# Two of a pixel's 36 deformable samples made on TensorE instead of one, their per-token rows spread over the partitions by transposes instead of by a trip through DRAM

## The reference, cut to what matters

```python
def bilinear_sample(img, iy, ix, H, W):
    x0, y0 = jnp.floor(ix), jnp.floor(iy)
    wx1, wy1 = ix - x0, iy - y0
    ...
    return corner(y0, x0, (1 - wy1) * (1 - wx1)) + corner(y0, x0 + 1, (1 - wy1) * wx1) \
         + corner(y0 + 1, x0, wy1 * (1 - wx1)) + corner(y0 + 1, x0 + 1, wy1 * wx1)
...
samp = bilinear_sample(img, iy, ix, Hin, Win).reshape(N, GROUP, H, W, P, Cg)
y = jnp.einsum('nghwpc,nhwgp->nhwgc', samp, mask_sm)      # P = 9 samples, masks by softmax
```

## Time and profile before

| | us |
|---|---|
| median of three runs | 8871.78 |
| the profiled execution | 8856.78 |
| its span in the profile | 8855.0 |
| TensorE matmul busy | 5535.4 |
| VectorE busy | 5200.9 |
| ScalarE busy | 2368.2 |
| GpSimd busy | 6546.0 |

### The profile page before, as it was taken

One profiled execution on the slowest core, in us unless ns is written; L12 is line 12 of the kernel. 1 busy time (PEld: TensorE's weight loads), 2 busy tenths in 40 slices (PEclk: granted clock), 3 DMA queues, 4 the chain that ended last, 5 costly groups with the idle time before them and its releaser, 6 DMA issues.

```text
span 8855.0 us, 69949 instructions
## 1 busy us (share of the span) xinstructions
PE 5535.4 (63%) x19826; PEld 3066.5 (35%) x19826; DVE 5200.9 (59%) x10762; ACT 2368.2 (27%) x5042; POOL 6546.0 (74%) x6899
## 2 busy tenths in 40 slices
PE   4547575656765577566675567664767566664567
PEld 2224343333432334333333334332433333332334
DVE  4655656556565655666475656655656655655553
ACT  2223222222332233222222222222323222222222
POOL 6777777777777777777777777777777777777771
PEclk7768787777877788777887778876878777776778
DMA  7323333233333323333233323333233323222220
GB/s 104 77 70 70 73 70 78 66 75 70 70 77 69 76 66 73 76 73 71 68 75 72 74 68 72 74 75 69 67 78 71 76 66 65 73 65 65 62 64 15
DMA packets 851804, 624.52 MB, mean 71 GB/s; under 512 B 551035, under 2 KB 734563, under 8 KB 851473
## 3 DMA queue, kind: packets, MB, share of 16 engines
q0 software_dynamic: 221200, 452.53, 21.1%
q1 hardware_dynamic: 629600, 167.72, 11.4%
q10 hardware_dynamic: 672, 0.24, 0.0%
HBM read 549.38 MB, written 70.57 MB: 70 GB/s over the span
## 4 chain that ended last, share of the span: by engine, by line
POOL 57%; issue 21%; PE 12%; DVE 6%; DMA 3%; SPq 1%; ACT 1%; POOLq 0%; DVEq 0%; another core or an unknown queue 0%; ACTq 0%
POOL ring L715 57%; PE bank L1466 2%; PE bank L1500 2%; PE bank L1488 2%; DMA ring<-column_table,idx_r 2%; DVE y L1042 2%; PE bank L1394 1%; PE bank L1651 1%; PE bank L1628 1%; DVE ring L1032 1%; PE bank L1563 1%; SPq L530 1%; DMA tokens<-z 0%; SPq L500 0%; DMA tin<-tokens 0%
## 5 line engine op out<-in xcount | busy, mean ns | idle before, releaser
L715 POOL DMA_INDIRECT ring<-column_table,idx_r x6860 | 6521.9, 951 | 2129.6 <-issue 2069.1
L1032 DVE TENSOR_TENSOR ring<-ring,bank 128x4608 f32<-128x4608 f32 x196 | 970.3, 4950 | 1189.4 <-POOLq L726 1188.2
L1042 DVE TENSOR_REDUCE y<-ring 128x128 f32<-128x4608 f32 x196 | 1572.9, 8025 | 24.3 <-remote 22.3
L1455 PE MATMUL bank<-ident,xh 112*128 112x112 f32 x224 | 56.4, 407 | 1317.0 <-DVE xh L962 1317.0
L1466 PE MATMUL bank<-kT,qT 128*112 128x448 f32 (+3 forms) x1792 | 812.8, 601 | 98.4 <-DVE cmax L1141 62.9
L1152 DVE RECIPROCAL rinv<-bank 112x2 f32<-112x2 f32 x112 | 18.5, 165 | 1307.0 <-PE bank L1513 1307.0
L1500 PE MATMUL bank<-pT,xh 112*128 112x448 f32 (+3 forms) x1792 | 774.2, 514 | 17.6 <-ACT pT L836 15.8
L1488 PE MATMUL bank<-qT,kT 128*112 128x448 f32 (+3 forms) x1792 | 750.4, 504 | 1.2 <-ACT qT L830 1.2
L836 ACT ACTIVATE pT<-bank 112x448 f32<-112x448 f32 (+3 forms) x896 | 451.7, 506 | 820.6 <-PE bank L1488 642.3
L1563 PE MATMUL bank<-xpad,diag 128*128 128x448 f32 x1008 | 492.0, 652 | 235.2 <-ACT xflat L853 184.1
L1141 DVE TENSOR_REDUCE cmax<-bank 112x1 f32<-112x448 f32 (+3 forms) x896 | 506.1, 579 | 187.3 <-PE bank L1466 94.3
(11 more groups left out here) (187 smaller groups left out, 7061.6 us busy)
## 6 DMA issues: line engine op xcount, KB each, us to landing
ring<-column_table,idx_r POOLq DMA_INDIRECT x6860
xflat<-dense_rows SPq DMA_DIRECT2D x56, 406.0 KB
column_table<-proj SPq DMA_DIRECT2D x196, 112.0 KB
corner_weight<-wts_s SPq DMA_DIRECT2D x56, 252.0 KB, 4.5
wts_r<-corner_weight SPq DMA_DIRECT2D x196, 72.0 KB
hT<-dense_rows SPq DMA_DIRECT2D x224, 56.0 KB
tin<-tokens SPq DMA_DIRECT2D x56, 224.0 KB, 3.1
out<-xn SPq DMA_DIRECT2D x56, 224.0 KB
```

What stands on the lines that cost most here:

```text
L715: pool.indirect_dma_start(ring[:, r, e * CORNERS:(e + 1) * CORNERS, :].rearrange("p s c -> p (s c)"), None, source, bass.IndirectOffsetOnA ...
L1032: dve.tensor_tensor(corners, corners, wts_p.unsqueeze(2).broadcast_to([128, GP * CORNERS, CG]), ALU.mult)\
L1042: dve.tensor_reduce(y[:, k % BLK % 2].rearrange("p (g c) -> p g c", g=G), ring[:, bass.ds(t % RING, 1)].rearrange("p o (g e) c -> p (o g) ...
```

## The change

FETCHED goes from 35 to 34 and DENSE = 2 samples of a pixel are made from image rows on TensorE, both of group 3. Ring buffers shrink to 136 corners. The multiply covers 128 x 4352 elements, and the sum is split in two instructions, groups 0 to 2 and group 3 with its 7 gathered samples. The trip through DRAM is gone (`store_rows`, `load_rows` and their semaphores): `drow` becomes a ring of LEAD = 8 chunks, `spread_rows` makes 16 transposes of single columns read with stride zero over 116 columns, and `widen_weights` (ScalarE) with `spread_weights` (TensorE, 4 transposes a sample) and `keep_weights_spread` (ScalarE) put the row weights on 128 partitions in `part`. There are now 10 items of two hats and two matmuls instead of 5. `keep_part` moves from `experts_front` to the end of `attention`.

```diff
-FETCHED = GP - 1
+DENSE = 2
+FETCHED = GP - DENSE
+STAGES = NB // 2
+ITEMS = DENSE * STAGES
 def hats_ahead(j):
-    return min(NB // 2 - 1, 2 + j)
+    return max(STAGES, ITEMS + 1 - blocks(j))
 # SyncE
-    load_rows(i, j, gd, fronts)          # in mlp
-    store_rows(i, j)                     # in front
 # ScalarE
+def widen_weights(gd, d):
+    act.wait_ge(d_placed, FIRST + gd + 1)
+    act.activation(t1[:, :, :].rearrange("p t (r c) -> p t r c", r=DY),
+                   drow[:, gd % LEAD, d, :, 2:].unsqueeze(3).broadcast_to([TT, NT, DY, CG]), ACT.Copy)
+def keep_weights_spread(p, f, d):
+    ...
+    act.activation(part[:, f % 2, d], bank[WEIGHT_BANK][:, 0:CH], ACT.Copy).then_inc(d_weights_kept, 1)
+    if d + 1 < DENSE:
+        widen_weights(gd, d + 1)
 # ScalarE, attention
-    for stage in range(ahead):
-        hats(gd, stage)
+    widen_weights(gd, 0)
+    for item in range(ahead):
+        hats(gd, item)
 ...
+    if now and b < DENSE:
+        keep_weights_spread(*now, b)
-    if now and 1 <= b <= NB // 2 - ahead:
+    if now and 1 <= b <= ITEMS - ahead:
         hats(gd, ahead + b - 1)
 # VectorE
+    for d in range(DENSE):
+        step.did(dve.tensor_scalar(place[d], bank[PLACE_BANKS[d][0]][0:2 * PAD, 0:CH], ...))
+    for d in range(DENSE):
+        step.wait()
+        ins = dve.scalar_tensor_tensor(place[d], place[d], -1.0, bank[PLACE_BANKS[d][1]][0:2 * PAD, 0:CH], ...)
-    if now: keep_part(*now)              # experts_front, behind the layer norm
+    if now: keep_part(*now)              # attention, ahead of the reads of o_projected; now two multiplies
 # TensorE
+def spread_rows(gd):
+    for d in range(DENSE):
+        for r in range(2):
+            for t in range(NT):
+                ins = pe.transpose(bank[PLACE_BANKS[d][r]][0:2 * PAD, t * TT:(t + 1) * TT],
+                                   rows[:, d, t, r:r + 1].broadcast_to([TT, 2 * PAD]), ident[0:TT, 0:TT])
+def spread_weights(gd, d):
+    for t in range(NT):
+        ins = pe.transpose(bank[WEIGHT_BANK][:, t * TT:(t + 1) * TT], t1[:, t, :], ident[0:TT, 0:TT])
 # TensorE, attention
     banks_left(fronts, s * 2 + h, g)
+    spread_rows(gd)
 ...
+    pe.wait_ge(d_placed, FIRST + gd + 1) # ahead of the scores
     for q in range(NT):
         ...                              # scores of q
-    sum_columns(di, gd, 0)
+        sum_columns(di, gd, q)
 ...                                      # row of maxima
-    for stage in range(1, ahead): sum_columns(di, gd, stage)
+    spread_weights(gd, 0)
+    for item in range(NT, ahead): sum_columns(di, gd, item)
 ...                                      # in the loop of turned scores, at block b
-        if now and 1 <= b < NB // 2 - ahead:
+        if now and 1 <= b <= ITEMS - ahead:
             sum_columns(di, gd, ahead + b - 1)
-    sum_columns(di, gd, NB // 2 - 1)     # behind the loop
+        if now and b + 1 < DENSE: spread_weights(gd, b + 1)
```

More of the change, by code:

```diff
@@ L154, in build @@
         stripes = sb("stripes", [2 * PAD, NB, DY * CG])
[L155 to L164, removed]
+        drow = sb("drow", [TT, LEAD, DENSE, NT, ROWS_KEPT])
+        dtmp = sb("dtmp", [TT, 4, DENSE, NT])
+        dint = sb("dint", [TT, DENSE, NT], I32)
+        part = sb("part", [128, 2, DENSE, CH])
+        wqT, wkT, wv_row = (part[:, 0, 0, k * C:(k + 1) * C] for k in range(3))
+        wqT_less, wkT_less = (part[:, 1, 0, k * C:(k + 1) * C] for k in range(2))
+        place = [hT[0:2 * PAD, d] for d in range(DENSE)]
+        ring = sb("ring", [128, RING, FETCHED * CORNERS, CG])
         x0 = ring[0:TT].rearrange("p r e c -> p (r e c)")[:, 0:NJ * NT * C]\
@@ L532, in load_stripes @@
                                      .rearrange("k x d -> x k d")).then_inc(d_stripes_in, 16)
[L534 to L543, removed]
-                sp.sem_inc(passed, 1)
-                sp.dma_start(xflat[0:2 * PAD].rearrange("p a n -> p (a n)"),
-                             row_d[gd, 0:2].rearrange("a n -> (a n)").partition_broadcast(2 * PAD)).then_inc(d_rows_in, 16)
-                for dy in range(DY):
-                    sp.dma_start(row_wts[dy * CG:(dy + 1) * CG], row_d[gd, 2 + dy].partition_broadcast(CG))\
-                        .then_inc(d_rows_in, 16)
             def dense(now):
-                load_rows(*dense_chunk(*now), (0, LEAD))
+                pass
             def first_image():
@@ L1148, in attention @@
                     sum_up(*second)
+                if now:
+                    keep_part(*now)
                 for a in range(2):
@@ L1398, in dense @@
                 i, _, gd = dense_chunk(*now)
-                for stage in range(NB // 2):
-                    sum_columns(i, gd, stage)
+                banks_left((0, LEAD), 0, 0)
+                spread_rows(gd)
+                for item in range(ITEMS):
+                    sum_columns(i, gd, item)
+                for d in range(DENSE):
+                    spread_weights(gd, d)
                 pe.wait_ge(d_kept, FIRST + gd + 1)
@@ L1479, in attention @@
                 if now:
-                    for stage in range(1, ahead):
-                        sum_columns(di, gd, stage)
+                    spread_weights(gd, 0)
+                    for item in range(NT, ahead):
+                        sum_columns(di, gd, item)
                 pe.wait_ge(row_kept, FIRST + g + 1)
```

163 lines of the change are left out of this document (97 added, 66 removed).

## The result

The changed kernel takes 8631.43 us, the median of 4 runs (8628.62 to 8636.41); the kernel before, beside it on the same chip, 8870.35 (8860.55 to 8876.0). The profiled execution took 8630.16 us, its span is 8628.4. All ratios here leave out two runs that lay far above the others of their kernel (12,087 us in experiment 4, 15,765 us in experiment 6).

The account below looks back on a forecast made before the run. The prediction took GpSimd's gathers, 188 tiles plus a tail, as the bound: 8855 - 235 + 22 + 1 = 8643 us for the span, -212; off the median, 8871.8 - 212 = 8660. Range 8640 to 8740.

Parts of the forecast that it names:

- 188 gathers at 1.25 us: GpSimd's stream: one gather fewer in each of the 188 tiles that count saves 235 us; by the reported span, 179.
- The tail, +22: From VectorE's last gather wait, tile 187, to the end: two dense chunks at +11.5 and +10.5 us; from +10 to +34.
- the places ahead of it: `set_places` on VectorE, ahead of the scores: reads PSUM, twice, 2.1 to 2.5 us instead of 1.1, so +1.4.
- The cover at tile 31: GpSimd's margin before tile 31: of 36 us, less some 3 for landing, 1 to 2 remain; waits +1 us in all.
- The copy's 4.2 us from the early `keep_part`: ScalarE's copy of the turned input, in fronts of 6 of 7 chunks, starts 4.2 us sooner without waiting for `keep_part`.
- VectorE's waits 330: VectorE's total wait for gathers over the kernel falls from 1188 us to some 330.
- What a tile costs beside its gathers (1.257 against 1.25 a gather) stays.: GpSimd's stream: the time per tile beyond its gathers' pitch was taken as unchanged.
- -10 us at an image's first chunk: SyncE's queue: without the removed loads, about 10 us (0 to 11) of VectorE's 13.26 us wait goes; the stripes stay.
- Taken off the median, 8871.8 - 212 = 8660.: Whole kernel: the -212 us change of the span was applied to the median, the profiled execution lying 15 us below it.
- a hidden tail: Rival: the first item falls into VectorE's lag at the scores' start; tail +5, no wait, 8643 us; chance 0.08.
- waits at tile 31: Rival: cover gone, waits of 6 to 26 us at tiles 31, 80, 129; 8680 to 8740 us; chance 0.27.
- The slow rival: ScalarE paces the loop and the engines behind the gathers become the bound: 25 us a chunk, 9067 us; chance 0.03.

Follow-up runs that it names:

- experiment 4: Changed kernel with one sample of a pixel from image rows and 35 gathered, by the new route: 8838.06 us, ratio 0.9972 to the kernel before.
- experiment 6: Twelve runs of variants of the changed kernel under conditions where every kernel took 13.9 to 14.6 ms; ratios to the kernel before from 0.9751 to 1.0245.
- Experiment 5: Changed kernel with 33 gathers a tile, sample 33 left out and its ring place zeroed once: 8447.92 us, ratio 0.9538 to the kernel before.
- experiment 3: Changed kernel with parts of the removed DRAM trip issued again, results unused: store alone 8678.82 us, ratio 0.9778; loads alone, from the input, 8650.65 us, ratio 0.9743.
- the whole trip: Changed kernel with the DRAM trip's store and loads issued again, result unused, and VectorE's wait for the store: 8691.35 us, ratio 0.9795 to the kernel before.

## Why the prediction was wrong, step by step

**Right.** *188 gathers at 1.25 us.* The spacing is 1.249 in the traces of before and after, and -234.8 us stands in the difference. The span (0.95 us) would have given 179; the gathers' start-to-start spacing is what counts.

*The tail, +22.* It is +22.5, and the tail of the kernel before, profiled twice, differs by 2.0 us itself (527.7, 529.7). Its terms can be read off the eight j = 3 chunks, as medians of the timeline: from the first score matmul to the last 16.0 us before and 22.6 after, +6.6 (forecast +4.6, and +1.4 for the places ahead of it); from there to the loop 7.1 and 4.8 (-2.4; forecast -2.2); the loop 24.6 and 34.0 (+9.4; forecast +9.5). That the loop would stay TensorE's, with ScalarE just under its pace, holds: 3.0 us an item. Part of the close total is luck: from the first query transpose of a chunk to that of the next, the first dense chunk of the tail grew by 14.4 us (forecast 11.5) and the second by 9.5 (10.5), while the last two, put at nothing, changed by -2.0 and +0.9. The 16 transposes of the rows took 1.7 us in 37 of 56 chunks and 3.2 in the three at a granted clock of 0.5 (forecast 2.3 to 4.0).

*The cover at tile 31: "1 to 2 us are left".* 3.5 are, from which the prediction's "some 3 for landing" are still to be taken: some 0.5, and one wait of 2.1 us in all, where +1 was taken. From tile 19, where VectorE last waits, to the freeing of the buffer at tile 27 it took 19.9 us more (436.1 to 456.0 us), forecast 17.5. The load then came 2.5 us sooner behind the freeing, without the store ahead of it. Experiment 5 shows that this margin decides what another step costs.

*The copy's 4.2 us from the early `keep_part`:* 3.8 by the traces, and the wait comes back when it is put back. What it is worth in the whole was not measured.

*VectorE's waits 330:* 390.

**Wrong.** *"What a tile costs beside its gathers (1.257 against 1.25 a gather) stays."* It does not: the loss of the stream beside the gathers falls from 54.6 to 39.2 us, 15.4 us, and the kernel with one sample and the new route has the same 39.3. 11 of the 15 us are the waits at sixth gathers, the landings of the tile before, which come shortly behind the store of single values and come back with it (12.0 us in experiment 3). The other 4 us are in the pauses of the stream and did not come back with the store or with the whole trip; their cause is open. The prediction had costed the removed trip on SyncE's queue alone (-10 us at an image's first chunk) and had counted neither its packets nor whose landings they share the DMA engines with. Even on the queue it saw only the loads: it wrote that the stripes stay, but issuing them, 19.98 us in the earlier trace rows, takes 13 to 14.5 us at each image in all four kernels without the store, and 16 to 21 from the second image on with it. After the change:

```profile
3128.21 13.41 SPq L531 DMA_DIRECT2D stripes<-column_table  x4
```

VectorE's waits for `tokens` behind it (5.7 to 13.3 us at four images) are gone, did not return with the loads alone, and did return with the whole trip (4.8 to 11.1 us at three images).

The rows gave reason to ask: 0.30 us and even is the pause inside a tile, while the window of the earlier trace rows holds 8273.2 - 6580 x 1.249 = 55 us beside it, which was called constant without asking what it was made of.

*"Taken off the median, 8871.8 - 212 = 8660."* This carried the 15 us between the profiled execution and the median over to another kernel. They went too: the changed kernel's profiled execution lies 1.3 us under its median, that of one sample by the new route 1.3 under, with the loads kept 1.1 above. With 33 gathers it is 1.7 under. The kernels with the store have theirs 11.5 (store alone), 5.9 (whole trip), 15.0 and 16.1 us (before, twice) below. So the median seems to hold a further loss by the store, one that the profiled execution does not show. That the gap goes with the store is seen in four kernels without it and three with it, on one profiled execution each but for before; why it does was not settled.

The two together are the whole miss: span 8643 forecast and 8628.4 found, -14.6; and 8660 - 8643 = 17 us of offset where 3 were found, -14. The lower end of the range, 8640, took in a hidden tail only and no gain of the stream. Both errors have the same sign, and both go with the store: most of the first is shown to come from it, the second only moves with it.

None of the rivals came. The one with a price nearest by, waits at tile 31, needed 2.1 us. ScalarE did not pace the loop. The slow rival needed 21 us a chunk; in the condition of experiment 6, where the consumer is the bound, the second sample costs it 10.7.

## What to carry to other kernels

Where a transfer is removed or added, count its packets, not its bytes, and ask which landings share the DMA engines with them and what stands behind them on their queue: here some 2700 four-byte packets a chunk cost a kernel 47 us when its cover was thin, most of it through the load that was next on the queue. Split a bound's time into pitch times count and the rest, and say what the rest consists of before calling it constant; and don't carry the distance between a profiled execution and the median over to a kernel that has other transfers. When work is traded from a bound to a nearly free set of engines, follow the cover at its thinnest place, and look there at what the load stands behind: the first step gained all of its 235 us less the tail, the next already 56 us less.

## What the runs showed of the hardware that was not expected

A transpose whose operand is one column read with stride zero over 116 columns costs about as much as another. The groups of the kernel after for it (`drow`), for the weights (`t`) and for the queries (`xh`, at a granted clock of 0.5), with busy us and mean ns of one:

```profile
L1413 PE MATMUL bank<-ident,drow 112*116 112x112 f32 x896 | 111.0, 284 | 116.7 <-issue 115.9 <-DVE proj L1188 0.9
L1422 PE MATMUL bank<-ident,t 112*128 112x112 f32 x448 | 64.7, 266 | 2.5 <-ACT t L797 2.5
L1503 PE MATMUL bank<-ident,xh 112*128 112x112 f32 x224 | 56.4, 408 | 973.7 <-DVE xh L967 973.7
```

16 of them in one run take 1.7 us at the full granted clock and 3.2 at 0.5, ahead of the layer norm, where they were expected to be covered. The new route as a whole lengthened the stretch from the queries' transposes to the last value product of a j = 3 chunk by only 1.5 us (51.8 before, 53.3 in experiment 4).

A store of 0.6 MB in 151,424 packets costs more than 36 MB of loads (47 us against 19). The next transfer on its queue takes 2.6 us to issue instead of 0.3, and the four loads of stripes some 20 instead of 14. The distance between the profiled execution and the median goes with the store.

And there is a condition in which all kernels take 57 to 68% longer while the multiply of a tile, say, takes its 4683 ns as ever; a comparison made in it has another bound, and can have another sign.
